# The gate product of the first expert layer, moved from GpSimd's queue to VectorE's

## The reference, cut to what matters

```python
x = x + L0_conv(ln_c(x))                       # windowed attention
t = to_tokens(x)
tokens = ln_t(t)
probs = softmax(tokens @ router_w.T)           # 8 experts, the best two kept, their weights normalised
out = tokens
for e in range(8):
    h = gelu(tokens @ w1[e] + b1[e])
    y = h @ w2[e] + b2[e]
    out = out + combine[:, e:e + 1] * y
t = t + out
x = x + L1_conv(ln_c(x))                       # 1x1 convolution, group norms, 2-d convolution, 1x1 convolution
t = t + L1_moe(ln_t(to_tokens(x)))             # 16 experts, top 2, gathered by expert
```

## Time and profile before

| | |
|---|---|
| median of 3 runs | 723.18 us (721.99, 725.02, 723.18) |
| profiled execution: its time, its span | 722.22 us, 720.4 us |
| PE busy | 557.8 us, 77% of the span |
| DVE busy | 356.0 us, 49% |
| ACT busy | 355.9 us, 49% |
| POOL busy | 424.4 us, 59%; 95.3 us of it are 96 gate products |
| chain that ended last | PE 59%, DVE 12%, POOL 10%, ACT 8%, issue 7% |
| dense steps | first GELU at 191.6 us, last sum of a group at 389.4 us |

### The profile page before, as it was taken

How to read it: one execution, slowest core, us unless ns; L and a number is a source line. 1 busy time by engine, 2 the same in 40 slices (tenths; PEclk the granted TensorE clock), 3 DMA queues, 4 the chain that set the end, 5 groups by cost and what they waited for, 6 DMA issues and landing times.

```text
span 720.4 us, 15997 instructions
## 1 busy us (share of the span) xinstructions
PE 557.8 (77%) x5352; PEld 462.0 (64%) x5353; DVE 356.0 (49%) x1040; ACT 355.9 (49%) x843; POOL 424.4 (59%) x484
## 2 busy tenths in 40 slices
PE   0477889679699999999996689736169999999900
PEld 0365767568377776677774467516069999999800
DVE  5877887844600612020014554582855555555523
ACT  0656778975754445751135523224036665666500
POOL 5587799864085686663342100077477777777771
PEclk9999999988988899999996689755579999999955
DMA  9342222211256353231490000011223333333636
GB/s 346 91 137 77 71 72 80 76 46 46 93 205 220 124 192 131 89 132 45 157 315 1 1 0 1 0 49 52 63 77 97 95 94 96 98 96 96 203 108 211
DMA packets 58319, 75.30 MB, mean 105 GB/s; under 512 B 9390, under 2 KB 48518, under 8 KB 57454
## 3 DMA queue, kind: packets, MB, share of 16 engines
q1 hardware_dynamic: 50894, 60.49, 26.4%
q0 software_dynamic: 5632, 11.62, 4.8%
q10 hardware_dynamic: 1728, 2.36, 0.9%
HBM read 57.96 MB, written 23.81 MB: 114 GB/s over the span
## 4 chain that ended last, share of the span: by engine, by line
PE 59%; DVE 12%; POOL 10%; ACT 8%; issue 7%; DMA 3%; SPq 1%; POOLq 0%; DVEq 0%; ACTq 0%
PE bank L797 13%; PE bank L759 9%; PE bank L858 8%; PE bank L742 8%; PE bank L808 7%; POOL gathered_or_att L567 3%; PE bank L719 3%; POOL padded_or_w L558 3%; PE bank L317 3%; ACT normed L903 2%; POOL returned L637 2%; DVE ln_stats L1088 2%; POOL gathered_or_att L576 2%; PE bank L788 2%; PE bank L757 1%
## 5 line engine op out<-in xcount | busy, mean ns | idle before, releaser
L602 POOL TENSOR_TENSOR padded_or_w<-padded_or_w,gathered_or_att 128x384 f32<-128x384 f32 x96 | 95.3, 999 | 88.8 <-ACT padded_or_w L976 73.1
L618 POOL DMA_INDIRECT sorted_x<-normed,slot x72 | 71.9, 999 | 97.5 <-DVE slot L1310 76.3
L637 POOL DMA_INDIRECT returned<-gathered_or_att,home_of_slot x104 | 103.3, 993 | 31.7 <-issue 22.3
L976 ACT ACTIVATE padded_or_w<-bank,moe_b 128x384 f32<-128x384 f32 x96 | 55.4, 580 | 99.2 <-PE bank L742 98.9
L759 PEld LDWEIGHTS bank<-moe_or_conv,padded_or_w 128*128 128x128 f32 x576 | 82.5, 201 | 31.8 <-issue 10.6
L759 PE MATMUL bank<-moe_or_conv,padded_or_w 128*128 128x128 f32 x576 | 85.8, 288 | 0.0
L742 PE MATMUL bank<-chan_major,moe_or_conv 128*128 128x384 f32 x192 | 81.1, 507 | 0.1
L990 ACT ACTIVATE att_or_moe<-bank 128x256 f32<-128x256 f32 x104 | 40.0, 384 | 56.8 <-PE bank L797 56.8
L1339 DVE TENSOR_TENSOR att_or_moe<-att_or_moe,bank 128x256 f32<-128x256 f32 x104 | 43.7, 420 | 48.9 <-PE bank L808 28.1
L808 PE MATMUL bank<-w,att_or_moe 128*128 x416 | 63.4, 276 | 0.8 <-ACT gathered_or_att L999 0.8
L657 PE MATMUL bank<-padded_or_w 64*64 64x64 f32 x1152 | 46.8, 231 | 21.2 <-issue 15.5
(11 more groups left out here) (178 smaller groups left out, 1091.9 us busy)
## 6 DMA issues: line engine op xcount, KB each, us to landing
gathered_or_att<-combine SPq DMA_DIRECT2D x24, 768.0 KB, 4.0
padded_or_w<-windows SPq DMA_DIRECT2D x192, 48.0 KB, 1.9
sorted_x<-in_pad_rows SPq DMA_DIRECT2D x26, 260.0 KB, 7.0
padded_or_w<-sorted_x SPq DMA_DIRECT2D x26, 260.0 KB
padded_or_w<-in_moe_w SPq DMA_DIRECT2D x8, 512.0 KB, 5.1
residual<-in_x_tok SPq DMA_DIRECT2D x2, 1152.0 KB, 6.1
qy<-returned SPq DMA_DIRECT2D x6, 384.0 KB, 7.5
out<-residual ACTq DMA_DIRECT2D x12, 192.0 KB, 2.1
```

Of the source, the lines that this page charges most:

```text
L602: nc.gpsimd.tensor_tensor(HB[n % DRING], HB[n % DRING], GB_[k % 3][:, n % 4, :], ALU.mult).then_inc(S("gated"), 1)
L618: nc.gpsimd.indirect_dma_start(xs_dram[b], bass.IndirectOffsetOnAxis(ap=POS[b][:, k, t:t + 1], axis=0), TNR[b][:, t, :], None).then_inc(S( ...
L637: nc.gpsimd.indirect_dma_start(yt_dram[b], bass.IndirectOffsetOnAxis(ap=HOMES[b][:, j:j + 1], axis=0), YR[k * RING + j % RING], None).then ...
L976: nc.scalar.activation(HB[n % DRING], banks[HBANK[n % 2]][:, 0:DG], ACT.Gelu, bias=B1C[:, e:e + 1]).then_inc(S("gelu"), 1)
```

## The change

The gate product leaves POOL's `dense`, which goes away with it, and becomes the first operation of DVE's `dense(n)`, ahead of `added`. The operation, its waits (the GELU, and at every fourth step the load of gates) and the semaphore that it raises stay the same. Nothing changes in the list of phases.

```diff
@@ POOL @@
-            def dense(n):
-                if n < DN:
-                    k = n // 4
-                    pool.wait_ge(S("gelu"), n + 1)
-                    if n % 4 == 0:
-                        pool.wait_ge(S(f"gates{k % 3}"), 16 * (k // 3 + 1))
-                    nc.gpsimd.tensor_tensor(HB[n % DRING], HB[n % DRING], GB_[k % 3][:, n % 4, :], ALU.mult).then_inc(S("gated"), 1)
-
...
-            run(A=lambda n: attend(att, n), AN=add_normed, D=dense, XC=pad, RS=scatter, M=send_back)
+            run(A=lambda n: attend(att, n), AN=add_normed, XC=pad, RS=scatter, M=send_back)
@@ DVE @@
             def dense(n):
+                if n < DN:
+                    k = n // 4
+                    dve.wait_ge(S("gelu"), n + 1)
+                    if n % 4 == 0:
+                        dve.wait_ge(S(f"gates{k % 3}"), 16 * (k // 3 + 1))
+                    tt(HB[n % DRING], HB[n % DRING], GB_[k % 3][:, n % 4, :], ALU.mult).then_inc(S("gated"), 1)
                 if n >= DLAG and (n - DLAG) % EX[0] == EX[0] - 1:
                     added((n - DLAG) // EX[0])
```

## The result

The changed kernel is slower: the ratio of its time to that of the kernel before is 1.0070, with a 95% interval from 1.0046 to 1.0093. Its median is 728.72 us (722.93 to 737.14, 20 runs) beside 722.04 us for the kernel before (715.22 to 727.03, 20 runs). The ratio leaves out the four longest runs of the changed kernel (734.34 to 737.14 us), which count as slow; by the two medians of all runs it would be 1.0093. Against the 723.18 us that the prediction started from, the ratio gives 728.2 us (726.5 to 729.9); predicted were 730.5, 726.5 to 735.

The account below looks back on a forecast made before the run. The prediction took PE to bound the dense steps. Terms of 1.2 (first product and early sums), 0.1, 3.6, 2.0 and 1.0 sum to 7.9 us, giving 730.1 or 731.1; it wrote 730.5 us, range 726.5 to 735.

Parts of the forecast that it names:

- First product: At the first load of gates: the product ends sooner on DVE and PE starts that much sooner, -0.44 us.
- Early sums: End of the attention: six POOL sums collide with DVE's routing, 2.1 us late, 1.6 us reaching the load of gates.
- Steady steps: Dense steps: lag of four steps hides DVE's products; the norm ahead of the convolution costs +0.1 us (0 to 0.5).
- Rival 2: Routing steps 20 to 28: DVE becomes the bound, PE loses about 2.5 us, 733 us; chance 0.07.
- Stall at step 63: Behind step 62: the product of step 63 stands behind DVE's whole group norm and PE waits, +3.6 us (3.3 to 3.9).
- Clock behind it: Behind the gap at step 63: PE's granted clock falls to 0.50 for a while, +2.0 us.
- rival 1: Stalls come, but the clock holds or DVE gets in between POOL's sums: 726.5 to 729 us; chance 0.16.
- Norm behind step 89: Product of step 90 behind the group norm: PE 2.3 us late, partly absorbed by an existing wait, +1.0 us.
- Rival 3: Faster: the shorter product and the end of DVE's collisions with POOL's products decide, 719.6 us; chance 0.03.

Follow-up runs that it names:

- x1: The changed kernel with the products of steps 63 to 67 and 90 to 93 back on POOL: 1.0001 to the kernel before, 722.48 us.
- x4: The changed kernel with DVE's group norms behind steps 62 and 89 each cut in three, products between the parts, sums still early: 0.9983 to the kernel before.
- x6: The kernel before with only the nine products behind the two norms on DVE: 1.0092, 727.85 us.
- x5: The changed kernel with both norms cut in three and POOL's sums behind each step's product: 0.9987 to the kernel before.
- y5: x5 once more, in a second comparison: 0.9979 to the kernel before.
- x3: The changed kernel with the nine products behind the norms back on POOL and POOL's sums behind each step's product: 1.0002 to the kernel before, 722.43 us.
- y7: The kernel before, all products on POOL, with six residual sums ahead of POOL's first product, in its second comparison: 1.0046.

## Why the prediction was right, and where it was not

The forecast, slower by the stall at step 63 and what follows, holds: `x1`, `x4` and `x6` show that in the changed kernel the nine products behind the two norms make the loss, and no others. Its sum of 7.9 us was too large; the ratio says 5.1 (3.3 to 6.7). That the total lies in the range is in part luck: in the profile (b) and (d) give back 3.9 and 3.1 us, which stood in no term. Term by term:

- **First product**, -0.44: right, 0.61 us against 1.05 from its start to PE's. In (a) it shows as 16.55 to 16.69 against 16.99 in three profiles, and not in `x5` and `y5`, where the first product itself started about 0.4 us later.
- **Early sums**, +1.6: the collision is as predicted, 2.1 us late, but the step that failed is that "about 0.5 of which was slack behind other matmuls". There is none: PE's matmul comes 0.14 us behind the end of DVE's L1175 (191.01 + 0.55 against 191.70), the operation behind the combine, and so all 2.14 us arrive. It was the same in the kernel before, where L1183, the same operation, ended 0.14 us ahead of the matmul at 189.97 us, as this row of its timeline shows. That (b) would then give some 4 us back, in both profiles of the changed kernel, was not in the sum at all.

```profile
189.28 0.55 DVE L1183 TENSOR_TENSOR residual<-residual,bank 128x384 f32<-128x384 f32 x1
```

- **Steady steps**, +0.1: right that nothing is to be seen; PE waits for no product but the first and the two behind the norms, and `x3` is 1.0002. Rival 2 is out.
- **Stall at step 63**, +3.6: 3.43 or 3.44 us in each of five profiles, inside 3.3 to 3.9. The chain was as described.
- **Clock behind it**, +2.0 (0 to 2.6): mis-sized. It lost nothing in both profiles of the changed kernel, as rival 1 had it, and 3.4 to 4.7 us, more than the bound, in three profiles of variants, where it stayed low for 7 to 10 us and not the 5.5 taken from the earlier trace rows. The window of the earlier trace rows begins behind that gap; the low stretch began in it and took about 7 us, from 150.3 to 157.2 us. How often the clock falls behind step 63 in the runs without a profile can't be read, as only its mean over a run is on record; the spread of the changed kernel, 722.93 to 737.14 us, has room for both.
- **Norm behind step 89**, +1.0: the gap is 2.12 us as worked out (2.3), but the step that took back 1.3 of it failed. PE's wait of 1.55 us ahead of `XU` was indeed absorbed, but the clock fell for 3.5 us just there (at 0.48 us lost in each microsecond an estimate of 1.7 us), and (c) shows both gaps whole: 99.00 - 93.29 = 5.71 against 3.43 + 2.12 = 5.55. It came back behind: from `XU` on the clock was up until PE's next wait, and (d) is 12.6 us. In the kernel before it was not, as one row of its timeline and then one of its windows show:

```profile
397.17 2.28 PE L873 MATMUL bank<-conv_mid,conv_w 32*128 32x288 f32 x4 [4.71 <-ACT chan_major L1054]
```

```profile
382.50:403.00 20.50, 15.21 (x47) 9.33 (x45) 10.85 (x32) 10.61 (x23) 6.27 (x7) 0.50 0.00 1
```

With these, the two profiles add up: the changed kernel's less that of before it is -0.41 at the start, +2.23 in (a), -3.86 in (b), +5.71 in (c), -3.07 in (d), together +0.60 us, which is 397.77 - 397.17. The other 2.5 us of the span lie behind, where nothing is changed; the mean granted clock there is 0.79 in the changed kernel's profile and 0.81 in that of before, and the same stretch takes from 322.0 us (`x5`) to 328.3 (`y7`) in the profiles. So one pair of profiles can show 3.1 us and the ratio of many runs 5: the gaps are fixed, and what the clock gives and takes around them is not. How the 5 us are shared out between gaps and clock over the runs without a profile stays open.

Rival 3, faster, came true in a way once the waits were out of the way: `x5` is at 0.9979 (0.9961 to 0.9997) in its second comparison, about 1.5 us under the kernel before, and 0.9987 in the first. It is the only version with an interval wholly below 1, in one comparison of two; its gain is about a fifth of a per cent, (c) has 0.2 us of it, and where the rest comes from stays open.

## What to carry to other kernels

Before an operation is moved to an engine that is faster and has room, look for the instructions of that engine that wait: what stands behind a wait in an in-order queue gets the wait as its price, however short it is itself, and cutting the waiting phase in pieces at the point of each wait takes that price away. Look as well at what the engine that is relieved will now start earlier, and what that collides with. Where the clock rises and falls with the gaps, two profiles differ by more than the gaps; compare distances between the same two instructions, stretch by stretch, before a difference of spans is explained.

## What was not expected of the hardware

The same gap of 3.4 us at step 63 was followed by 7 to 10 us at half clock in three profiles and by none in two, while the shorter gap of 2.12 us was followed by about 3.5 us of it in all five. A start of the dense steps that came 2.2 us later was followed, with the products on DVE, by a path that was 4 us shorter in three of four profiles, and in that of `x1`; in the one of them whose windows stand above, 7 us of it were at half clock, and 17 in `x7`.
